# Wide attention on one core: query and key products behind the sums and three pairs ahead, output projection waiting pair by pair

## What is computed

```
q = (x @ Wq).reshape(b, s, 16, 64);  k, v likewise
dot = einsum('bihd,bkhd->bhik', q, k)
w = softmax(dot / sqrt(64), axis=-1)
a = einsum('bhij,bjhd->bihd', w, v).reshape(b, s, 1024)
x = x + a @ Wo + bo                      # a, q, k, v from layernorm(x)
```

## Time and profile before

| | |
|---|---|
| median of 3 runs | 2408.94 us (2400.86 to 2410.99) |
| profiled execution | 2402.08 us, its span 2400.2 us |
| TensorE busy over the span | 2097.6 us (87%) |
| VectorE | 1555.6 us (65%) |
| ScalarE | 1197.1 us (50%) |
| GpSimd | 762.4 us (32%) |
| mean granted TensorE clock | 0.930 |

### The profile page before, as it was taken

How to read it: one execution, slowest core, us unless ns; L and a number is a source line. 1 busy time by engine, 2 the same in 40 slices (tenths; PEclk the granted TensorE clock), 3 DMA queues, 4 the chain that set the end, 5 groups by cost and what they waited for, 6 DMA issues and landing times. The chain is left out here.

```text
span 2400.2 us, 52498 instructions
## 1 busy us (share of the span) xinstructions
PE 2097.6 (87%) x20671; PEld 1388.0 (58%) x20671; DVE 1555.6 (65%) x2742; ACT 1197.1 (50%) x2044; POOL 762.4 (32%) x1208
## 2 busy tenths in 40 slices
PE   4999999999968997889769989998589996469996
PEld 2566666666656896555558976665344543335553
DVE  3777777777744434666354446775688884868883
ACT  3444444444343333666633325565467776437774
POOL 3444444444403231333021314441133321423330
PEclk9999999999969998999779999999689997669998
DMA  5000000000000021444000104452244430134441
GB/s 163 1 1 1 1 1 1 1 1 1 1 1 6 5 54 39 114 110 118 8 4 1 41 15 110 110 118 50 56 105 105 110 74 1 26 86 112 111 104 47
DMA packets 142786, 120.95 MB, mean 50 GB/s; under 512 B 11808, under 2 KB 127408, under 8 KB 142548
## 3 DMA queue, kind: packets, MB, share of 16 engines
q1 hardware_dynamic: 142548, 117.64, 20.6%
HBM read 63.48 MB, written 54.12 MB: 49 GB/s over the span
## 5 line engine op out<-in xcount | busy, mean ns | idle before, releaser
L906 DVE TENSOR_REDUCE l_group_mx<-maxima 128x4 f32<-128x1024 f32 x248 | 304.0, 1226 | 72.3 <-PE maxima L699 70.6
L834 ACT ACTIVATE l_group_pr<-scores 128x1024 f32<-128x1024 f32 x256 | 261.5, 1021 | 71.0 <-PE scores L720 68.7
L2134 POOL TENSOR_TENSOR l_wide_tiles_sum<-l_wide_pr 128x256 f32<-128x256 f32 x256 | 180.5, 726 | 359.5 <-ACT l_wide_pr L2077 359.5
L2105 DVE RECIPROCAL l_wide_rc<-bank 128x256 f32<-128x256 f32 x128 | 224.4, 1753 | 56.7 <-PE bank L2041 55.7
L2077 ACT ACTIVATE l_wide_pr<-scores 128x512 f32<-128x512 f32 x256 | 138.9, 595 | 226.0 <-PE scores L2024 226.0
L2089 DVE TENSOR_REDUCE l_wide_mx<-maxima 128x2 f32<-128x512 f32 x248 | 159.4, 685 | 32.5 <-PE maxima L2004 32.5
L906 DVE TENSOR_REDUCE l_slope_mx<-maxima 128x6 f32<-128x768 f32 x124 | 118.9, 959 | 77.6 <-PE maxima L706 76.1
L906 DVE TENSOR_REDUCE l_rope_mx<-maxima 128x6 f32<-128x768 f32 x124 | 118.8, 958 | 57.0 <-PE maxima L706 56.0
L834 ACT ACTIVATE l_slope_pr<-scores 128x768 f32<-128x768 f32 x128 | 103.5, 809 | 90.3 <-PE scores L727 90.1
L740 PE MATMUL bank<-l_group_pr,va 128*32 128x256 f32 x2048 | 143.6, 400 | 0.0
L834 ACT ACTIVATE l_rope_pr<-scores 128x768 f32<-128x768 f32 x128 | 103.7, 810 | 77.4 <-PE scores L727 77.2
(11 more groups left out here) (460 smaller groups left out, 4859.0 us busy)
## 6 DMA issues: line engine op xcount, KB each, us to landing
l_group_st<-stack_dram SPq DMA_DIRECT2D x64, 384.0 KB, 5.5
l_slope_st<-stack_dram SPq DMA_DIRECT2D x32, 384.0 KB, 5.5
l_rope_st<-stack_dram SPq DMA_DIRECT2D x32, 384.0 KB, 5.5
stack_dram<-l_group_parts SPq DMA_DIRECT2D x64, 192.0 KB, 2.3
stack_dram<-l_group_parts SPq DMA_DIRECT2D x64, 128.0 KB, 1.9
stack_dram<-l_slope_parts SPq DMA_DIRECT2D x32, 192.0 KB, 2.4
stack_dram<-l_rope_parts SPq DMA_DIRECT2D x32, 192.0 KB, 2.3
stack_dram<-l_slope_parts SPq DMA_DIRECT2D x32, 128.0 KB, 2.3
```

Of the source, the lines that this page charges most:

```text
L834: act.activation(pr[:, i % AHEAD, :, 0:keys], Tp[:, :, 0:keys], ACT.Exp).then_inc(s["exps"], 1)
L906: dve.tensor_reduce(mx[:, b % 2, :, :, i], max_bank(i, b)[:, :, 0:BLOCKS * keys].rearrange("p z (a k) -> p z a k", k=keys), AX.X, ALU.max, ...
L2105: own.done(dve.reciprocal(rc[:], Ob[i % 2][:, S:2 * S]))
L2134: pool.tensor_tensor(tiles_sum[:, i % 2, z, :], pr[:, i % 2, z, 0:S], pr[:, i % 2, z, S:2 * S], ALU.add).then_inc(s["added"], 1)
```

## The change

In `wide_slots`, the query and key products go behind value and sums of the slot, with the slot's other filler behind them; only in slot 7 they stay ahead. They belong to the pair three further on and no longer two. The transposes of the maxima go behind the maxima in slot 7. The norm moves from slot 5 to 4, its ScalarE part from 3 to 2, the value projections from slots 1, 2, 3, 5 to 1, 2, 4, 6, and the output projections from slots 4 and 6 to 3 and 5. In the output projection, the wait for all eight divided pairs becomes one for six pairs ahead of the first matmul and one for each of the last two.

```diff
@@ wide_slots
         slot = [("divide", (i - 2) % PAIRS, -1 if i < 2 else 0), ("score", i, 0)]
-        slot += [("turnmax", 0, 1)] if i == 7 else []
         slot += [("max", (i + 1) % PAIRS, 2 if i + 1 >= PAIRS else 1)]
         slot += [("split", 0, 1)] if i == 6 else []
-        slot += [("qk", (i + 2) % PAIRS, 2 if i + 2 >= PAIRS else 1)]
-        slot += [(what, (i - 1) % PAIRS, -1 if i < 1 else 0) for what in ("value", "sum")]
-        slot += {1: [("v", 0, 1)], 2: [("v", 1, 1)], 3: [("v", 2, 1), ("xn", 0, 2)], 4: [("project", 0, -1)],
-                 5: [("v", 3, 1), ("norm", 0, 2)], 6: [("project", 1, -1)]}.get(i, [])
-        slots += slot
+        slot += [("turnmax", 0, 1)] if i == 7 else []
+        products = [("qk", (i + 3) % PAIRS, 2 if i + 3 >= PAIRS else 1)]
+        products += {1: [("v", 0, 1)], 2: [("v", 1, 1), ("xn", 0, 2)], 3: [("project", 0, -1)],
+                     4: [("v", 2, 1), ("norm", 0, 2)], 5: [("project", 1, -1)], 6: [("v", 3, 1)]}.get(i, [])
+        values = [(what, (i - 1) % PAIRS, -1 if i < 1 else 0) for what in ("value", "sum")]
+        slots += slot + (products + values if i == 7 else values + products)
@@ wide_attention, TensorE
                 elif what == "project":
-                    pe.wait_ge(s["divided"], PAIRS * (b + 1))
                     for c in range(PAIRS):
+                        if c >= PAIRS - 2:
+                            pe.wait_ge(s["divided"], PAIRS * b + c + 1)
+                        elif c == 0:
+                            pe.wait_ge(s["divided"], PAIRS * b + PAIRS - 2)
                         ins = pe.matmul(bank[:, 0:C], att_t[:, at, c, i * P:(i + 1) * P], W["wo"][:, c, :],
```

## The result

The changed kernel takes 2378.2 us in the median of four runs (2372.21 to 2384.28) against 2404.9 for four runs of the kernel before: ratio 0.9892, 95% interval 0.9854 to 0.993. It is faster by 1.1%. The forecast was 2385 with a range of 2370 to 2401. The profiled execution took 2376.45 us, its span is 2374.7.

What follows compares the result with a forecast made beforehand. TensorE's start-to-start timeline was taken as the bound. Savings of 14.1 (fourteen rounds), 1.4 (round 14), 4.8 (opening) and 3.8 (end), 24.1 us, took 2402.08 to 2378.0; with 6.9 for the median, 2385, range 2370 to 2401.

Steps and rivals of the forecast that it cites:

- Part 1: Slots with an extra projection: full-shape work in one piece saves 0.20 us each, six slots, 1.20 us per round.
- Part 2 and 3: Slot 7: transposes behind maxima save TensorE 0.21 us; VectorE's later shift copy makes score 0 wait 0.40 us per round.
- Part 4: Opening rounds: products three pairs ahead hide GpSimd's casts; 4.8 us saved, bounds 3 and 8.5; worth nothing in steady rounds.
- the bank waits: Opening: successive fillers sharing a bank wait for ScalarE's copy, counted as 0.76 + 0.76 + 0.2 us.
- My upper bound, 8.5: Opening's largest saving in us: none of the new waits, 9.6 idle less 1.06 for one more query/key product.
- Part 5: Round 14, with only the next batch's items: four slots save 0.20, one product is gone, longer shift wait; 1.4 us saved.
- Part 6: Output projection waiting pair by pair: added waits taken as free, last projections start earlier and run faster; 3.8 us saved.
- the last sign that I had named for being wrong: A later layer whose granted clock falls in other places would show the prediction wrong; no size given.
- One charge: Rival: shape changes cost once per slot, so each slot saves only 0.10 us; 2394 us, chance 0.17.
- charges only moved: Rival: shape-change charges move to new neighbours (maxima to value, sums to query), saving 9.2 us; 2400 us, chance 0.13.
- the slow case: Rival: VectorE's chain in slots 6 and 7 becomes the bound; with 3 us of wait 2421 us, chance 0.05.
- The rival without a wait: GpSimd's cast misses VectorE's split, leaving 0.04 of score 0's 0.40 us wait; 2380 us, chance 0.15.

Runs made afterwards that it cites:

- experiment 1: Kernel before, with each slot's extra filler put directly behind the query and key products, ahead of value and sums: ratio 0.9922, round 38.88 us.
- experiments 7 and 8: Changed kernel, one engine altered each: VectorE copies the shift ahead of the reductions; GpSimd's cast waits for VectorE's split. Round 38.63 us in both.
- experiment 6: Changed kernel with the transposes of the maxima ahead of the maxima again in slot 7: round 38.88 us against 38.91.
- experiment 2: Kernel before with products three pairs ahead instead of two, norm moved as needed: first score 47.66 us, round 40.01; timed again, ratio 0.9968.
- experiment 5: Changed kernel with products two pairs ahead again, still behind the sums: round 39.37 us, first score 54.61.
- experiment 4: Kernel before with only the output projection's wait split by pairs: round 40.02 us; first score to next layer's first matmul 631.15 against 635.50.
- The three parts alone: Kernel before with one step each: 128x128 work in one piece; products three pairs ahead; projection waits by pairs. Next layer's first matmul 674.14, 681.88, 685.16 us.
- banks by turns: Changed kernel with each filler's bank alternating over work that really runs, not by list place: first score 42.82 us, 3.6 earlier.
- the run with the filled start: Changed kernel with 150 and 28 unused small transposes filling TensorE's idle time ahead of the opening's products: first score 47.01 us, 0.6 later.

## Why the prediction was right

**Bound and Part 1: right, with the right cause.** TensorE's timeline set the end and the 0.20 per slot came within 0.01 (4.96 to 4.77), in the change and alone (experiment 1). Reading two places where the same pair of instructions stands with and without a change of shape was enough. The bound of 0.10 more for maxima to value wasn't needed.

**Part 2 and 3: right, a little too dear.** The round without the wait is 38.63 (experiments 7 and 8), that is 1.38 under 40.01, where 1.41 was walked. The wait itself was 0.28 and not 0.40, because VectorE's steps from the split to the copy overlapped more than I let them (8.98 against 9.14). Both causes that I named, the order and the cast over the split, were each undone, and each alone removes it. Those 0.28 are by the rounds; the row of the wait has 0.22. What I hadn't seen is that part 2 is then worth nothing as it stands (experiment 6).

**Part 4: mechanism right, size wrong: 8.27 for 4.8.** The first score alone varies by up to 2.7 us with an unchanged opening, so the size is rough. The waits for the cast went completely, and the bank waits came (1.4 for 1.7). The terms that were off: The norm's copy held a query product for 0.46 (the changed kernel's timeline at 40.72) and not for 1.0, and the transposes didn't wait for the split (0.3); above all I left the speed of the matmuls out of the sum: they run at half speed in the opening, to 38 us before and to 30 after. Counted from the first product to the first score, idle time fell by 7.0 us (9.13 to 2.10), where I had 5.9, and busy time by 1.3 (23.85 to 22.57), where I had it grow by 1.06 for the added query and key product: of the 3.5 us missed, 1.1 are idle time and 2.3 are speed. My upper bound, 8.5, was made from idle time alone and holds only by luck. The sentence that three ahead is worth nothing in the steady rounds was wrong for the changed kernel: in the old order it is so (40.01 in experiment 2), but behind the sums it holds off a wait of 0.46 a round (experiment 5). The sum didn't suffer, as the change made both steps at once; that is luck too.

**Part 5: right.** 1.49 for 1.4, the wait at its end 0.52 by the row for 0.7.

**Part 6: right.** The waits are free, 4.61 for 3.8: 4.35 are the full speed behind the shorter gap (experiment 4). The other 0.26 may come from the earlier projections; no run isolates them.

**Sum and total.** The wide attention gained 30.3 for 24.1. The total of the profiled executions fell by 25.6, nearer to the forecast than the parts are, because 4.8 us went the other way in layers that vary by more than that from one execution to the next. That closeness is luck. It also answers the last sign that I had named for being wrong, a granted clock that falls elsewhere in later layers: its mean behind the mark was 0.90 and 0.91 in two executions of the changed kernel, so it was no sign. By the medians of both kernels timed together it is 26.7. The three parts alone (16.0, 8.3 and 4.4 by the end mark, the last from the first score) add to 28.7 of the 30.3. Even so they are not independent: with the products behind the sums, taking the third pair away costs 16.6 us (experiment 5), twice the 8.3 that it gives alone.

**Rivals.** One charge (39.4 a round) and charges only moved (40.0) fell with experiment 1; the slow case, decided from 2.1 us of wait on, had 0.28. The reason that I gave against it held: the split's first piece, 0.745 us at the median before, has 0.195 now, as GpSimd's addition is over at 308.52 and the split starts at 309.14. In a steady round of the kernel before that piece ran under the addition and ended 0.05 us behind it (323.97 and 323.92). The rival without a wait gave 2380, nearer to the median of 2378.2 than my 2385, but its mechanism did not come: the wait is there in every steady round.

## What to carry to other kernels

- Before moving matmuls for the sake of waits, look what stands next to what: the same pair of instructions at two places of the timeline, start to start, shows what a change between row-tiled, column-tiled and full shapes costs. Putting the full ones in one piece gave 16 of 30 us here with no other change.
- A list that orders all engines alike need not do so: a short copy that another engine waits for goes ahead of long reductions nobody waits for, on its own engine alone.
- Judge a part by a mark at the end of its stage. Totals of single executions differed by 10 us for one program.

## What the hardware showed that I had not expected

- 128x128 f32 work that has another shape on both sides pays about 0.20 us more (0.10 entering, 0.10 leaving), at full speed: 1.06 against 0.86 for the 512 columns of the value projection.
- Removing 5.6 + 2.4 us of holes brought full speed 8 us sooner; the speed, at 0.54 against 1.01 us for a query product, was then worth more than the holes in the last step (banks by turns: 2.9 of the 3.5 us from first product to first score are busy time, 0.7 idle time).
- The speed in the opening is read from durations (a query product has 1.22 or 0.70 us in its row). The granted clock of the busy table says 1.00 for all of 20.5 to 54.67 us of the kernel before, though its products there took 1.22 up to 34 us. In the run with the filled start the table shows both levels: 0.50 (1.2 GHz) from 23.01 to 25.70 beside a product of 1.22, and 1.00 (2.4 GHz) from 30.45 on beside 0.70.
- TensorE filled with small transposes for 10.6 us and then idle for 3.08 us came to its products at half speed. In a second run with the same filling and a gap of 2.73 us, the first product was at full speed and those up to 28 us were not.
